# A fused cross-attention and self-attention block: the prologue of the first batch rearranged, and new orders for the engines' steps

## What is computed

```python
# x, ctx: (4, 512, 512) float32; layernorm over the last axis; 16 heads of 32
def block128(t, eps):              # fp8 with one scale for each 128 (x: 1x128, ctx: 128x128)
    safe = max(absmax over the block, eps)
    return (t * (448 / safe)).astype(float8_e4m3fn) * (safe / 448)
x = x + tanh(g_xattn) * einsum("emk,enk->emn", block128(layernorm(x)), block128(ctx))
h = layernorm(x)
fused = h @ (Wa * col_scale)       # Q (24 of 32 rows a head), K, V, and 8 low rows of Q and K
Q, K: low rows swapped for heads with w_rec > 0.1
y = softmax(causal(Q K^T / sqrt(32))) V, for each batch and head
x = x + tanh(g_ffn) * (y @ Wp)
```

## Time and profile before

| | us |
|---|---|
| median of 3 runs | 502.21 (500.25 to 502.68) |
| the profiled execution | 499.74 |
| its span (first to last instruction) | 497.9 |
| PE busy in the span | 440.6 (88%) |
| DVE busy | 340.3 (68%) |
| ACT busy | 255.7 (51%) |
| POOL busy | 151.1 (30%) |
| mean granted TensorE clock | 0.977 of full |

### The profile page before, as it was taken

The page is one execution under the profiler, slowest core; times in us unless marked ns, Lnnn a source line. Parts: engine busy times, 40 slices in busy tenths (PEclk is TensorE's granted clock), DMA queues, the critical chain, the costliest instruction groups (busy, mean ns, idle before and its releaser), DMA issues.

```text
span 497.9 us, 7913 instructions
## 1 busy us (share of the span) xinstructions
PE 440.6 (88%) x2536; PEld 317.1 (64%) x2536; DVE 340.3 (68%) x1122; ACT 255.7 (51%) x498; POOL 151.1 (30%) x278
## 2 busy tenths in 40 slices
PE   0375989998979999998969999999879999999996
PEld 0352767775536788775535788776545788776764
DVE  5999627889994254889995253789995246556633
ACT  1695356566646450667645642466654424554530
POOL 5678474343225200343213400243122101121110
PEclk9998799999989999999999999999998999999999
DMA  7402173323500346223500234424400243234102
GB/s 225 197 1 87 39 246 82 91 69 96 146 2 2 89 101 193 67 56 95 141 27 0 64 97 127 138 53 98 97 11 2 58 102 97 64 95 102 60 21 86
DMA packets 27929, 42.62 MB, mean 86 GB/s; under 512 B 8272, under 2 KB 8528, under 8 KB 27888
## 3 DMA queue, kind: packets, MB, share of 16 engines
q1 hardware_dynamic: 25872, 41.18, 29.6%
q10 hardware_dynamic: 1824, 0.54, 0.6%
q0 software_dynamic: 192, 0.39, 0.3%
HBM read 12.59 MB, written 4.19 MB: 34 GB/s over the span
## 4 chain that ended last, share of the span: by engine, by line
PE 66%; DVE 24%; ACT 3%; issue 3%; DMA 2%; POOL 1%; SPq 0%; ACTq 0%; DVEq 0%; POOLq 0%
PE pv_bank L748 13%; DVE x_all L1201 10%; PE mm_bank L594 9%; PE mm_bank L595 8%; PE mm_bank L596 8%; PE exp_bank L734 6%; PE max_bank L717 5%; DVE max_bank L1230 5%; PE mm_bank L775 2%; PE mm_bank L777 2%; PE mm_bank L776 2%; PE turn_bank L610 2%; DVE bn L1208 2%; PE pv_bank L757 1%; DMA x_all<-in_x 1%
## 5 line engine op out<-in xcount | busy, mean ns | idle before, releaser
L1230 DVE CUSTOM_DVE_ANT_0 max_bank<-max_bank,causal 128x512 f32<-128x512 f32 (+3 forms) x256 | 121.0, 512 | 52.5 <-PE max_bank L717 52.0
L1002 ACT ACTIVATE work<-exp_bank 128x512 f32<-128x512 f32 (+1 forms) x192 | 94.9, 526 | 56.2 <-PE exp_bank L734 55.2
L512 POOL TENSOR_SCALAR_AFFINE_SELECT work<-work 128x384 f32<-128x384 f32 x64 | 33.4, 522 | 281.6 <-ACT work L1002 281.6
L748 PE MATMUL pv_bank<-work,v_aug 128*33 128x256 f32 (+3 forms) x512 | 78.9, 451 | 0.6 <-DVE work L1241 0.2
L734 PE MATMUL exp_bank<-q_stack,k_stack 97*128 97x512 f32 (+3 forms) x256 | 71.2, 341 | 7.6 <-ACT work L1002 6.5
L717 PE MATMUL max_bank<-k_stack,q_stack 96*128 96x512 f32 (+3 forms) x256 | 71.1, 338 | 2.4 <-DVE row_max L1230 1.8
L1201 DVE SCALAR_TENSOR_TENSOR x_all<-mm_bank,coef,x_all 128x128 f32<-128x128 f32 x224 | 61.5, 342 | 0.3
L748 PEld LDWEIGHTS pv_bank<-work,v_aug 128*33 128x33 f32 x512 | 29.7, 113 | 50.1 <-issue 42.1
L734 PEld LDWEIGHTS exp_bank<-q_stack,k_stack 97*128 97x128 f32 x256 | 45.6, 188 | 23.4 <-ACT work L1002 14.7
L594 PE MATMUL mm_bank<-xt_hi,w_hi 128*128 128x512 f32 x128 | 53.4, 417 | 0.7 <-ACT v_aug L981 0.7
L717 PEld LDWEIGHTS max_bank<-k_stack,q_stack 96*128 96x128 f32 x256 | 45.2, 191 | 12.7 <-DVE row_max L1230 3.7
(11 more groups left out here) (168 smaller groups left out, 789.1 us busy)
## 6 DMA issues: line engine op xcount, KB each, us to landing
q_stack<-qk_hi SPq DMA_DIRECT2D x128, 64.0 KB, 2.0
k_stack<-qk_hi SPq DMA_DIRECT2D x120, 64.0 KB, 2.0
x_all<-in_x SPq DMA_DIRECT2D x16, 256.0 KB, 3.6
ctx_raw<-in_ctx SPq DMA_DIRECT2D x16, 256.0 KB, 3.9
q_stack<-qk_lo SPq DMA_DIRECT2D x64, 64.0 KB, 2.0
out<-x_all SPq DMA_DIRECT2D x16, 256.0 KB, 2.4
k_stack<-qk_lo SPq DMA_DIRECT2D x60, 64.0 KB, 2.0
work<-in_L_ffn_Wa SPq DMA_DIRECT2D x3, 768.0 KB, 9.7
```

Source lines behind the costliest of these rows:

```text
L512: pool.affine_select(out=three, in_=three, compare_op=ALU.is_ge, fill=0.0, base=0, pattern=[[0, 3], [1, P]], channel_multiplier=-1)
L748: last = pe.matmul(pv_bank[64 * j:64 * j + D + 1, P * m:T], v_aug[:, m, 2 * u + j, :], prob[j][:, PROB_COL[m]:PROB_COL[m] + T - P * m], st ...
L1002: act.activation(prob[j][:, UNIT_COL[k]:UNIT_COL[k] + UNIT_LEN[k]], exp_bank[(3 * j + k) % 2][:, 0:UNIT_LEN[k]], ACT.Exp, scale=SCALE).the ...
L1230: last = dve.tensor_tensor_reduce(max_bank[unit % 2][:, col:col + width], max_bank[unit % 2][:, col:col + width], causal[:, T - width:T], ...
```

## The change

The prologue:

- ctx is loaded ahead of x. The three small loads on ACT's queue (w_rec and the two gates) are issued after ACT's first activations, and the eight loads of w_std and w_rec move to SP's queue, behind Wa.
- The fourth row block of Wa goes elsewhere: its V and low parts to `x_all`, its Q/K part into the place of the first block, after POOL's first `j0`. The layernormed x of the prologue lies in `v_aug` instead of `qk_lo`, so the ones in `v_aug` are set later.
- The fourth block sum of each row tile (`S3`, `S7`, `S11`, `S15`) is no longer added by DVE: ACT multiplies it by the coefficients (`s0`..`s3`, `first_product`) and POOL adds the product to x (`a0`..`a3`).
- The turned ctx tiles (`f0`..`f3`) are copied by DVE (`first_ctx`) instead of ACT.
- The scales of x are made for two tiles at a time (`G0`, `G1`), apart from the maxima (`F`).
- The first maxima (`M0`..`M5`) use `qk_hi` and `qk_lo` directly, three matmuls for each tile where one from the stacks stood, and no longer wait for the stacking DMAs.

All tables have new orders, also those of the steps of every batch, of the ends and of the last batch; apart from the prologue the items are the same, some of them in a neighbouring string.

```diff
 PE_STEPS = [
...
-    "S11 max0 rowmax max1 pv S12 max2 S13 max3 H0 S14 exp0 exp1 max4 exp2 H1 exp3 exp4 S15 exp5 max5 back",
-    "max0 rowmax max1 A0 pv exp0 H2 max2 exp1 exp2 max3 max4 exp3 exp4 max5 exp5 back",
...
+    "max0 rowmax max1 S12 H0 S13 pv exp0 exp1 max2 S14 max3 exp2 S15 max4 back H1 exp3 max5 exp4 exp5",
+    "rowmax max0 A0 max1 pv max2 exp0 H2 exp1 exp2 max3 exp3 exp4 max4 back exp5 max5",
...
-PE_FIRST = ("f0 f1 f2 f3 f4 S0 S1 S2 S3 f5 S4 S5 S6 f6 S7 S8 f7 S9 f8 S10 S11 S12 S13 S14 "
-     "S15 f9 f10 v0 f11 v1 q0 B0 B1 k0 V2 q1 M0 k1 M1 M2")
...
-POOL_FIRST = ("i0 s0 s1 s2 s3 s4 s5 o0 s6 j0 s7 r0 j1 l0 l1 r1 l2 l3 r2 r3 j2 j3 g0 g1 "
-     "D0 g2 D1 g3 p0")
...
+PE_FIRST = ("f0 f1 f2 f3 f4 f5 S0 S1 S2 S3 S4 S5 f6 S6 S7 S8 f7 S9 S10 S11 f8 S12 S13 f9 "
+     "S14 S15 v0 v1.0 f10 v1.1 f11 v1.23 q0.0 B0 q0.123 B1 k0 V2 M0 M1 q1.012 M2 q1.3 M3 M4 k1 M5")
+
+ACT_FIRST = ("a0 a1 C0 C1 b0 C2 d0 C3 C4 C5 f4 f5 C6 b1 s0 C7 f6 s1 a2 e3 a3 f7 b2 N0 "
+     "s2 N1 f8 s3 b3 f9 v0 N2 N3 f10 f11 q0 v1 p0 k0 c0 V2 D0 D1 c1 q1 c2 k1 c3")
+
+DVE_FIRST = ("t0 t1 t2 w0 t3 x0 x1 A0 x2 x3 A1 T0 L0 L1 F0 L2 F1 F2 L3 G0 F3 f0 f1 T1 "
+     "G1 f2 f3 T2 c0 T3 S0 S1 S2 S4 S5 S6 b0 S8 b1 S9 S10 S12 h0 S13 S14 b2 h1 b3 "
+     "u0 u1 u2 h2 h3 u3 B0 B1 q0 k0 M0 M1 M2 q1 M3 M4 M5 k1")
+
+POOL_FIRST = ("i0 s0 s1 s2 s3 l0 s4 s5 o0 s6 s7 j0 l1 a0 j1 a1 r0 v0 r1 l2 l3 a2 j2 a3 "
...
-        late_raw = qk_hi[:].bitcast(FP32).rearrange("p g w t -> p (g w t)")[:, 0:NF]
-        raw_w = [work[:, 0:NF], work[:, NF:2 * NF], work[:, 2 * NF:3 * NF], late_raw]
...
-        first_x = qk_lo[:].bitcast(FP32).rearrange("p g w t -> p (g w) t")
+        first_x = v_aug[:].rearrange("p i h e -> p i (h e)")[:, :, 0:C]
...
+            load_ctx(0)
             load_tiles(0, 0)
-            load_ctx(0)
             wa_v = wa.rearrange("(k p) f -> p k f", p=P)
-            for k in range(NK):
+            for k in range(NK - 1):
                 sp.dma_start(raw_w[k], wa_v[:, k, :]).then_inc(s_wload[k], 16)
+            sp.dma_start(raw_v[NK - 1], wa_v[:, NK - 1, V0:LOW0]).then_inc(s_wload[NK - 1], 16)
+            sp.dma_start(raw_low[NK - 1], wa_v[:, NK - 1, LOW0:NF]).then_inc(s_wload[NK - 1], 16)
+            for j in range(H // NK):
+                std = w_std.rearrange("(g j) -> j g", j=H // NK)[j, :]
+                rec = w_rec.rearrange("(g j) -> j g", j=H // NK)[j, :]
+                sp.dma_start(col_root[D * j:D * j + DS, :], std.partition_broadcast(DS), allow_slow_non_contiguous=True).then_inc(s_small, 16)
+                sp.dma_start(col_root[D * j + DS:D * j + D, :], rec.partition_broadcast(R), allow_slow_non_contiguous=True).then_inc(s_small, 16)
+            sp.wait_ge(s_wlo, 1)
+            sp.dma_start(raw_qk[NK - 1], wa_v[:, NK - 1, 0:V0]).then_inc(s_wqk, 16)
             sp.wait_ge(s_cast, 2 * NT)
...
-                        pool.wait_ge(s_xscale, k - NT + 1)
+                        pool.wait_ge(s_xscale, (k - NT) // 2 + 1)
...
+                elif kind == "a":
+                    pool.wait_ge(s_fmul, i + 1)
+                    pool.wait_ge(s_summed, 3 * i + 3)
+                    pool.tensor_tensor(x_tile(0, i), x_tile(0, i), tile_buf[:, i, :], ALU.add).then_inc(s_fadd, 1)
...
-                    pe.wait_ge(s_summed, NK * i + k - NK + 1)
+                    if k == NK - 1:
+                        pe.wait_ge(s_fmul, i)
+                    else:
+                        pe.wait_ge(s_summed, 3 * i + k - 2)
...
+            def first_scores(unit):
+
+                j, k = unit // 3, unit % 3
+                if unit == 0:
+                    pe.wait_ge(s_const, 3)
+                    pe.wait_ge(s_summed, 12)
+                    pe.wait_ge(s_fmul, NT)
+                    pe.wait_ge(s_qklo, 2)
+                if unit >= 2:
+                    pe.wait_ge(s_max, unit - 1)
+                rows = slice(D * j, D * j + D)
+                for i, col in MAX_UNITS[k]:
+                    width = P * (i + 1)
+                    dst, cols = max_bank[unit % 2][:, col:col + width], slice(P * i, P * i + P)
+                    pe.matmul(dst, qk_hi[rows, 0, 0, cols], qk_hi[rows, 0, 1, 0:width], start=True, stop=False)
+                    pe.matmul(dst, qk_lo[rows, 0, 0, cols], qk_hi[rows, 0, 1, 0:width], start=False, stop=False)
+                    last = pe.matmul(dst, qk_hi[rows, 0, 0, cols], qk_lo[rows, 0, 1, 0:width], start=False, stop=True)
...
+            def first_product(i):
+                act.wait_ge(s_coef, 1)
+                act.wait_ge(s_turn, i + 1)
+                act.wait_ge(s_cross, NK * i + NK)
+                for t in range(NT):
+                    last = act.activation(tile_buf[:, i, P * t:P * t + P], sum_bank(True, i, NK - 1)[:, P * t:P * t + P],
+                                          ACT.Copy, scale=coef[:, i, t, NK - 1:NK])
+                last.then_inc(s_fmul, 1)
...
-            def first_scales(i):
+            def first_maximum(i):
                 dve.wait_ge(s_xn, i + 1)
...
-                scales(x_amax[:, i, :], x_up[:, i, :], x_down[:, i, :], ACT_EPS).then_inc(s_xscale, 1)
+
+            def first_scales(pair):
+                two = slice(2 * pair, 2 * pair + 2)
+                scales(x_amax[:, two, :], x_up[:, two, :], x_down[:, two, :], ACT_EPS).then_inc(s_xscale, 1)
...
-                dve.wait_ge(s_summed, 16 * n + NK * i + NK)
+                if n == 0:
+                    dve.wait_ge(s_fadd, i + 1)
+                else:
+                    dve.wait_ge(s_summed, 16 * n - NT + NK * i + NK)
...
+            def first_ctx(p):
+                dve.wait_ge(s_turn, p + 1)
+                dve.tensor_copy(wt_hi[:, :, P * p:P * p + P],
+                                first_bank(p)[:].rearrange("p (k c) -> p k c", k=NK)).then_inc(s_fctx, 1)
```

175 lines of the change are left out of this document (90 added, 85 removed), and 91 rows, old and new, of tables (ACT_LAST, ACT_STEPS, BEFORE, BEFORE_LATE).

## The result

The changed kernel takes 504.36 us (median of 13 executions), the kernel before beside it 501.46 (13 executions). The ratio is 1.0057, with a 95% interval of 1.0038 to 1.0075: 2.9 us slower, where I had forecast 4.4 us faster. One of the 13, of 2085 us, is left out of the ratio. The profiled execution took 502.42, its span is 500.7.

The account below looks back on a forecast made before the run. It took PE to bound the batches, except DVE in steps 3 to 5, and DVE much of the prologue. The prologue gains 4.4 us, the step orders 0: 499.74 less 4.4 is 495.3, plus 2.47 to the median, 497.8; range 493.3 to 500.9.

Parts of the forecast that it names:

- the 78.8 of my sum: Prologue: forecast time of `exp0`, against 83.69 before; a gain of 4.9, less 0.45 for PE's shifted work.
- The start of the sums: Prologue: with ctx loaded first, DVE's block sums start at 31.5 instead of 31.68, bounds 30.0 and 32.7.
- From the last sum to Q: Prologue, last block sums to first Q product: Q begins at 56.2 instead of 59.70, 3.5 us earlier.
- the slack that I gave POOL: POOL between 31 and 56: 5 or 6 us of slack for 3.5 us more work.
- the rule that I weighed: Two-SBUF-input DVE instructions or fast copies wait out POOL's SBUF-reading ones; charged nothing for the new additions, 1 us in range.
- From Q to the first exponentials: Prologue: Q to turned maxima takes 18.3 us, so maxima turned at 74.5 against 79.97, `exp0` gaining 4.9.
- The new orders of the steps: 0: Batches: reordered steps change no time; PE's waiting is split but its sum stays, and the clock likely falls too.
- my own sign of being wrong: Batches: the prediction is wrong if they differ from 115 us by more than 1.5.
- the third: Rival, prologue: POOL holds `b3` and weights' rests, Q no earlier, gain about 1; within the lesser-prologue case of 0.18.
- a case that ends at 500.5: Lesser prologue: clock stays at half into V and Q, one product loses 2.7 us: 500.5; chance 0.18.
- The slower rival: Steps: less work between `rowmax` and `exp0` makes PE wait; at 0.3 us in each of 32 steps, 507.4; chance 0.08.

Follow-up runs that it names:

- t3_late: Changed kernel with DVE's weight tail T3 moved from ahead of the block sums to ahead of `b3`, and ACT's `b3` behind `f9`: 501.30 us, 1.0007 to the kernel before.
- adds_dve: t3_late with the four additions of x and product moved from POOL to DVE, each ahead of its layernorm statistics: 501.26 us, 1.0010 to the kernel before.
- new_orders: Kernel before with the changed kernel's step, end and last-batch tables, without the new prologue: 500.38 us, 0.9984 to the kernel before.
- old_orders: Changed kernel with the step, end and last-batch tables of the kernel before, so the new prologue alone: 502.54 us, 1.0029 to the kernel before.
- a_early: t3_late with ctx's scales on DVE ahead of x's statistics and POOL's `s0`, `s1` ahead of `i0`: 503.36 us, 1.0060 to the kernel before.
- mend: Changed kernel with ctx's scales and scalings early, `a3` on DVE, `b2` ahead of `S14`, T3 behind `b3`: 503.89 us, 1.0062 to the kernel before.
- mend_mix: mend with the step orders of the kernel before in the first three batches, new ones in the last: 503.07 us, 1.0049 to the kernel before.
- mend4: mend with `h1` ahead of T3, w_rec and gates at ACT's start, old step orders in three batches, x ahead of ctx, POOL reordered: 499.75 us, 0.9970 to before.

## Why the prediction was wrong

`exp0` came at 85.09, 6.3 us later than the 78.8 of my sum. 4.0 of these are in place when the block sums start, 0.2 come between there and Q, and 2.2 between Q and the turned maxima. From `exp0` to the end the profiled execution took 1.4 more than that of the kernel before, where I had 0.45.

**The failed step is "The start of the sums".** I gave 31.5 with bounds of 30.0 and 32.7; it was 35.55. Of the 4.0 us, 2.8 are T3, which stands in DVE's changed order between `c0` and `S0` and was in no term of my sum. In the kernel before a tail like it takes 0.73 (T1, below), so the rest of the 2.8 is POOL's rest `j0` beside it. t3_late confirms the term: sums 2.6 us nearer to `i0`, 2.5 us of time, which is nearly all that the changed kernel had lost. 1.2 is the later `s0` and norm: 15.86 instead of 14.7. The last tile of x landed at 12.38, where the last of ctx had landed at 11.63 before, and the statistics behind it took 0.3 us longer, POOL's `i0` 0.2. The way from `s0` to the sums without T3, 16.9 against my 16.8, came out right in part by luck: the coefficients took 2.29 instead of 3.59, and the tails T1 and T2 4.3 instead of 1.5. I had costed the moved small loads at nothing, asking only when they would land themselves; what they do to the large loads beside them was in no bound (0.5 to 2.3 us at the eighth tile). w_rec itself landed at 6.74 and held nothing up, as I had said.

**"From the last sum to Q"** came out in length: from the start of the sums to Q 24.9 us, against 24.7 in my sum. `a3` ended at 54.42 instead of 50.4, and Q came at 60.42 instead of 56.2, each by the 4 us that the sums were late. What doesn't hold is the slack that I gave POOL, 5 or 6 us for 3.5 more of work: between 31 and 56 it was busy 17.0 us before and is busy 21.9 now, and from `a0` on it has no idle time. Still adds_dve shows that taking this work away frees nothing, for DVE is as full.

DVE is full because the sums it lost are made up for by others. The three instructions of T1 take 2.9 us in the changed kernel, those of T3 2.8. In the kernel before T1 stood beside only small instructions of POOL, of 128x4 elements:

```profile
26.53 0.28 DVE L1257 COPY x_all<-work 128x256 f32<-128x256 f32 x1
26.84 0.31 DVE L1259 COPY_PREDICATED x_all<-x_all,work 128x128 f32<-128x128 uint32 x1
```

That is 0.73 for the whole tail there. So the rule that I weighed, and put at up to 1 us on the sums, came at another place: the sums, which read a bank, are as fast beside POOL's additions as before (2.15 for eight), but SBUF-to-SBUF copies of 0.3 take 0.7 to 1.8. POOL beside T1 and T3 in the changed kernel:

```profile
24.38 1.04 POOL L518 TENSOR_TENSOR v_aug<-v_aug,x_up 128x512 f32<-128x512 f32 x1
...
32.81 1.93 POOL L539 TENSOR_TENSOR w_lo<-work,w_hi 128x768 fp32r<-128x768 f32 x1
34.70 0.78 POOL L541 TENSOR_TENSOR w_lo<-x_all,w_hi 128x256 fp32r<-128x256 f32 x1
```

The copy of 1.15 ends 0.14 after the first of these, the predicated copies of 1.79 and 0.82 end 0.16 and 0.15 after the other two. The Trainium skill (SBUF — State Buffer, Who interferes with whom) says this, that only instructions on the shared port wait, and for the whole of the other's instruction; the traces agree in both parts for POOL's instructions of 128x256 and more. They don't for the small ones: beside the 128x4 one that ran from 26.99 for 1.04 us in the kernel before, the copies kept their 0.3. I had applied it to the new additions alone and not to the copies that the new order puts beside POOL.

**"From Q to the first exponentials"**, to the turned maxima, was 18.3 and measured 20.5. PE is busy 20.4 of them. The last 1.0, from 79.97 on, are scores of the next step, done while DVE reduces the last maxima; they lie where I had 0.9 of waits. The other 19.5 hold the matmuls that I counted at 17.4: the products took 15.1 instead of 14.0, the maxima 4.5 instead of 3.4, for each change from one kind to the next costs. The rows of the kernel before held the same 2 us: PE was busy 17.23 of its 20.27 there, where I had counted 15.1 of work and taken most of the rest for waits that the change would save. The end of V2 and the start of M0 on PE:

```profile
69.05 0.39 PE L613 MATMUL mm_bank<-w_hi,xt_lo 128*128 128x512 f32 x1
69.37 0.49 PE L739 MATMUL max_bank<-qk_hi 32*128 32x512 f32 x1
69.70 0.39 PE L740 MATMUL max_bank<-qk_hi,qk_lo 32*128 32x512 f32 x1
```

One follows the other here after 0.32 and 0.33, where within a product it is 0.23; the changed order changes between products and maxima seven times, and the three short matmuls of 128 columns in M1 take 0.37 until `q1` starts, 0.17 by their columns. The way from the maxima to `exp0` was 4.13 instead of 4.3, with 0.71 of waiting for the DMA of neg_max.

**"The new orders of the steps: 0"** was right for the time within what can be told (new_orders 0.9984). Right was also that the clock still falls; wrong that it would be as before: in the profiled execution the stretches ahead of step 6 are twice as long, and 3.4 us more of half clock went with 1.0 and 0.5 us more in old_orders' first two batches (115.71 and 115.83 against 114.75 and 115.33). The batches of 116.85 and 116.32 are my own sign of being wrong: one differs from 115 by more than 1.5.

**The rivals.** The nearest is the third, that the change does not do what it says because of POOL, which I had folded into a case that ends at 500.5; my range ended at 500.9. Q indeed starts no earlier than before, but not by its cause: adds_dve takes the additions from POOL and gains nothing. None of them had the sums 4 us late. The slower rival's mechanism (waits ahead of `exp0`) is there, 1.1 us of PE's waits for the DMA of neg_max in the first batch, and is not what decided.

**What stays open:** how the small loads slow the large ones (the traces show that, not why), why executions of the changed kernel scatter more (from 500.56 to 507.28, the kernel before beside it from 499.86 to 503.36), which kernels such as old_orders with the same prologue do not (501.75 to 504.75), why the clock of one kernel falls for longer in some executions, and whether the new step orders cost 1.4 us on the new prologue.

## What to carry to other kernels

Write out, for each engine, every instruction that stands between two marks in the new order, and price it beside its new neighbours; one tail of three instructions left out of such a list was 2.8 us. Slack of an engine is worth only what lies at the place where the new work goes, and when two engines are full, relieving one gives nothing. Ask of a small load what it does to the large ones beside it: here 0.5 to 2.3 us at the last tile, of the 4.3 that the four saved sums were worth. A load that is moved ahead gains nothing by itself: here `s0` stayed behind x's statistics, and where it was moved ahead of them too (a_early), the norms came later.

## What the runs showed of the hardware

- An 8 KB broadcast and two of 0.5 KB, issued 1.3 us later among eight tiles of 256 KB, made the eighth tile land 0.3 to 2.5 us later (12.13 to 13.96 in twelve kernels against 11.45 to 11.82 in eight, one profiled execution each).
- DVE's four coefficient instructions of 128x16 took 1.46 us in mend, 2.29, 3.59 and 4.36 in others: the same work, and each time the last of them ended 0.03 to 0.2 us after one of POOL's.
- The granted clock can fall while PE works without a break. In mend_mix it fell at 79.06, after PE had been busy for all of the 16.16 us from Q on. In mend4 it was at half from 74.82 to 78.23, inside a stretch in which PE was busy 21.85 of 22.00 us:

```profile
58.48:80.48 22.00, 21.85 (x90) 16.34 (x89) 7.96 (x27) 11.36 (x18) 14.34 (x15) 0.92 0.60 184
74.82:78.23 3.41, 3.41 (x10) 2.63 (x9) 1.54 (x7) 1.03 (x2) 2.45 (x1) 0.51 0.30 74
```
